# Moving the first tile's output projection out of the mixing block and into attention's last two steps

## The reference, cut to what matters

```
x = x + xattn(layernorm(x), ctx, ctx, Wq, Wk, Wv, Wo)   # 32 batches, 32 queries, 257 keys, 32 heads (8 kv heads), D = 1024
x = x + attn(layernorm(x), eta)                          # "mixing": softmax(max - y y^T) y, per batch, scaled by eta
x = x + ffn(layernorm(x), gate_w, expert_w)              # 8 experts, the best 2 for each token
# inside xattn, after the heads:
out = (probs @ v).reshape(32, 32, 1024)                  # called oT in the kernel, kept transposed
return out @ Wo                                          # 1024 x 1024, the projection that the change moves for the first 128 rows
```

## Time and profile before

| what | value |
|---|---|
| median of 3 runs | 1096.29 us (1095.58 to 1100.33) |
| the profiled execution, time | 1093.26 us |
| the profiled execution, span from first to last instruction | 1091.7 us |
| busy: PE, PEld, DVE, ACT, POOL | 1051.1, 964.5, 632.9, 477.7, 245.2 us |
| mean granted TensorE clock | 0.985 |
| block 1 ends, block 2 starts | 708.3 us |

### The profile page before, as it was taken

The page is one execution under the profiler, slowest core; times in us unless marked ns, Lnnn a source line. Parts: engine busy times, 40 slices in busy tenths (PEclk is TensorE's granted clock), DMA queues, the critical chain, the costliest instruction groups (busy, mean ns, idle before and its releaser), DMA issues. The chain is left out here.

```text
span 1091.7 us, 25345 instructions
## 1 busy us (share of the span) xinstructions
PE 1051.1 (96%) x9020; PEld 964.5 (88%) x9021; DVE 632.9 (58%) x1626; ACT 477.7 (44%) x1127; POOL 245.2 (22%) x414
## 2 busy tenths in 40 slices
PE   9999989999999999999999999499998799999996
PEld 9999889999999999999999999377776688888885
DVE  6641256666667666666667666648777635245220
ACT  4321245555555555554555554513323345355331
POOL 2000211211212121212112121024545333232232
PEclk9999999999999999999999999699999999999999
DMA  9442566575757565675657555464537588588432
GB/s 341 136 154 79 185 185 183 173 204 163 207 149 210 169 184 171 181 199 172 198 154 212 162 154 134 162 216 117 98 78 262 123 267 234 172 268 237 137 75 37
DMA packets 78602, 189.45 MB, mean 174 GB/s; under 512 B 16512, under 2 KB 27136, under 8 KB 74400
## 3 DMA queue, kind: packets, MB, share of 16 engines
q1 hardware_dynamic: 64096, 154.15, 45.4%
q0 software_dynamic: 14400, 33.88, 13.1%
HBM read 148.66 MB, written 44.56 MB: 177 GB/s over the span
## 5 line engine op out<-in xcount | busy, mean ns | idle before, releaser
L451 ACT ACTIVATE prob<-bank,nmax 128x257 f32<-128x257 f32 x256 | 122.0, 477 | 244.6 <-DVE nmax L590 244.4
L590 DVE TENSOR_REDUCE nmax<-bank 128x1 f32<-128x257 f32 x256 | 108.8, 425 | 160.2 <-PE bank L790 160.2
L670 PE MATMUL bank<-cT_h,wkv_h 128*128 128x256 f32 x512 | 155.0, 303 | 0.0
L679 PE MATMUL bank<-wkv_h,cT_h 128*128 128x256 f32 x512 | 154.4, 302 | 0.0
L670 PE MATMUL bank<-cT_h,wkv_l 128*128 128x256 f32 x512 | 145.0, 283 | 0.0
L670 PE MATMUL bank<-cT_l,wkv_h 128*128 128x256 f32 x512 | 144.7, 283 | 0.0
L679 PE MATMUL bank<-wkv_h,cT_l 128*128 128x256 f32 x512 | 144.5, 282 | 0.0
L679 PE MATMUL bank<-wkv_l,cT_h 128*128 128x256 f32 x512 | 143.9, 281 | 0.0
L345 POOL DMA_DIRECT2D qcat<-q_scratch x128 | 70.2, 555 | 271.6 <-PE bank L790 268.6
L705 PE MATMUL bank<-ident,prob 128*128 128x128 f32 x512 | 101.4, 280 | 10.0 <-DVE pT L245 6.8
L1640 PE MATMUL bank<-w_h,rows_h 128*128 x272 | 107.4, 395 | 0.0
(11 more groups left out here) (210 smaller groups left out, 2395.9 us busy)
## 6 DMA issues: line engine op xcount, KB each, us to landing
kcat<-k_scratch SPq DMA_DIRECT2D x128, 258.0 KB, 4.1
cx<-in_context SPq DMA_DIRECT2D x32, 1024.0 KB, 7.4
raw<-in_expert_w SPq DMA_DIRECT2D x48, 512.0 KB, 7.6
qcat<-q_scratch POOLq DMA_DIRECT2D x128, 128.0 KB, 3.2
k_scratch<-kT_h SPq DMA_DIRECT2D x32, 258.0 KB, 2.6
k_scratch<-kT_l SPq DMA_DIRECT2D x32, 258.0 KB, 3.0
x_in<-in_x SPq DMA_DIRECT2D x16, 512.0 KB, 6.2
expert_raw<-in_expert_w SPq DMA_DIRECT2D x16, 512.0 KB, 8.9
```

The lines of the kernel that those rows point to most:

```text
L451: act.activation(prob[:, 1 - par, s, 0:SK], s_ps[s % 2][:, 0:SK], ACT.Exp, bias=nmax[:, 1 - par, s:s + 1], accum_out=sums[:, 1 - par, s:s ...
L590: dve.reduce_max(nmax[:, 1 - par, s:s + 1], s_ps[s % 2][:, 0:SK], AXX, negate=True).then_inc(max_done, 1)
L670: o = pe.matmul(k_ps[:, j * 256:(j + 1) * 256], wkv[w][:, k, j * P:(j + 1) * P], cT[t][:, b % 2, k, :], start=(j == 0 and k == 0 and n == ...
L679: o = pe.matmul(v_ps[:, a * KV:(a + 1) * KV], cT[t][:, b % 2, k, a * P:(a + 1) * P], wkv[w][:, k, KV:2 * KV], start=(a == 0 and k == 0 and ...
```

## The change

1. TensorE makes `product` of tile 0 in block 1, in `first_product(k)`: chunk k of Wo is multiplied for both halves of the output at once (6 matmuls), one chunk in each of the slots (32, 3), (32, 4), (32, 5), (32, 6), (33, 0), (33, 1), (33, 2), (33, 3). Block 2 starts with tile 1.
2. The split of oT's tiles 0 and 1 (`ot_high`, `ot_low`) moves into block 1: tile 0 in (32, 1) on ScalarE and (32, 2) on VectorE, tile 1 in (33, 4) on both, behind the copy of the last batch into oT.
3. Wo's chunks 0 to 2 are loaded at step 28 and split in (30, 2), (30, 6), (31, 2) (ScalarE; VectorE a slot later). Chunks 3 to 7 are split in (32, 4), (32, 6), (33, 0), (33, 1), (33, 2).
4. For the last batch ScalarE copies five turned groups (1, 3, 4, 6, 7) instead of three.
5. The loads of x for tiles 0 and 1 move from SP's list in block 2 to the end of its list in block 1.
6. Buffers are laid out anew so that all this fits. The only waits that this adds to the steps before are one of GpSimd for `vl_zeroed` ahead of the first step.

The core of the diff:

```diff
+def turned_by_scalar(a):
+    return (1, 3, 4, 6, 7) if a == B - 1 else (1, 4, 7)
+def wo_step(c):
+    return ((B - 2, 2), (B - 2, 6), (B - 1, 2), (B, 4), (B, 6), (B + 1, 0), (B + 1, 1), (B + 1, 2))[c]
+def product_step(c):
+    return ((B, 3), (B, 4), (B, 5), (B, 6), (B + 1, 0), (B + 1, 1), (B + 1, 2), (B + 1, 3))[c]
...
 (SP, block 1)
+                if b == B - 4:
+                    for c in range(EARLY_WO):
+                        load_wo(c)
...
+            sp.wait_ge(v_done, B - 1)
+            for c in range(EARLY_WO, KC - 1):
+                load_wo(c)
+            for part in range(2):
+                sp.wait_ge(k_stored[part], 16 * B)
+            load_wo(KC - 1)
             sp.wait_ge(cT_done, 4 * B)
-            for c in range(KC // 2):
-                load_wo(c)
-            sp.wait_ge(v_done, B)
-            for c in range(KC // 2, KC):
-                load_wo(c)
+            for t in range(2):
+                sp.dma_start(sh.x_in2[:, t, :], x[t * P:(t + 1) * P, :]).then_inc(sh.x2_loaded[t], 16)
...
 (ScalarE, end of a slot)
-                    c = (b - B) * NG + s - 2
-                    if 0 <= c < KC:
-                        act.wait_ge(v_done, B)
-                        act.wait_ge(chunk_loaded[c], 32)
-                        act.activation(wo_s[0][:, c, :], wo_loaded(c), ACT.Copy).then_inc(wo_h_ready, 1)
+                    for c in range(KC):
+                        if wo_step(c) == (b, s):
...
+                            act.wait_ge(chunk_loaded[c], 32)
+                            act.activation(wo_s[0][c][:, :], wo_raw[c][:, :], ACT.Copy).then_inc(wo_h_ready, 1)
+                    if (b, s) in ((B, 1), (B + 1, 4)):
+                        t = b - B
+                        act.wait_ge(s_done, NG * (B - 1))
+                        act.activation(sh.ot[0][:, t, :, :], oT[:, t, :, :], ACT.Copy).then_inc(sh.ot_h_ready, 1)
...
 (VectorE, end of a slot)
+                    for c in range(KC):
+                        if wo_step(c) == (b, s - 1):
+                            dve.wait_ge(wo_h_ready, c + 1)
+                            dve.tensor_tensor(wo_s[1][c][:, :], wo_raw[c][:, :], wo_s[0][c][:, :].bitcast(F32), ALU.subtract).then_inc(wo_l_ready, 1)
+                    if (b, s) in ((B, 2), (B + 1, 4)):
+                        t = b - B
+                        dve.wait_ge(turned, NG * (B - 1))
+                        dve.wait_ge(sh.ot_h_ready, t + 1)
+                        dve.tensor_tensor(sh.ot[1][:, t, :, :], oT[:, t, :, :], sh.ot[0][:, t, :, :].bitcast(F32), ALU.subtract).then_inc(sh.ot_l_ready, 1)
...
 (TensorE)
+            def first_product(k):
+                if k == 0:
+                    pe.wait_ge(sh.ot_l_ready, 1)
+                    pe.wait_ge(cT_l_ready, 4 * B)
+                pe.wait_ge(wo_l_ready, k + 1)
+                for h in range(2):
+                    for m, (a, b) in enumerate(PASSES):
+                        o = pe.matmul(banks[h][:, :], sh.ot[a][:, 0, k, :], wo_s[b][k][:, h * 512:(h + 1) * 512],
+                                      start=(k == 0 and m == 0), stop=(k == KC - 1 and m == 2))
+                    if k == KC - 1:
+                        o.then_inc(sh.xo_done, 1)
...
+                    for c in range(KC):
+                        if product_step(c) == (b, s):
+                            first_product(c)
...
 (block 2)
-            load_x(0)
-            load_x(1)
...
-            ot_high(0)
             for t in range(NT + 2):
-                if t + 1 < NT:
+                if 1 <= t and t + 1 < NT:
                     ot_high(t + 1)
...
-            for t in range(NT):
+            for t in range(1, NT):
                 for unit in range(KC):
```

More of the change, by code:

```diff
@@ L65, in __init__ @@
         self.oT = self.at("oT", HIGH0, [P, NT, KC, P])
-        self.wo = [self.at("wo_h", HIGH1, [P, KC, D], F32R), self.at("wo_l", LOW1, [P, KC, D], F32R)]
+        place = lambda c: LOW1 + 8 * D * (c + 1) if c < EARLY_WO else LOW1 if c == KC - 1 else HIGH1 + 8 * D * (c - EARLY_WO)
+        self.wo = [[self.at(f"wo_{part}{c}", place(c) + i * 4 * D, [P, D], F32R) for c in range(KC)] for i, part in enumerate("hl")]
+        self.rows = [self.at("rows_" + part, STAGE + 16 * D + ROWS_AT + i * 8 * D, [P, 2, D], F32R) for i, part in enumerate("hl")]
+        self.ot = [part[:, :, :].rearrange("p a (c n) -> p a c n", n=P) for part in self.rows]
+        self.x_in2 = self.at("x_in2", STAGE, [P, 2, D])
+        self.x2_loaded = [sem("x2_loaded0"), sem("x2_loaded1")]
+        self.ot_h_ready, self.ot_l_ready, self.xo_done = sem("ot_h_ready"), sem("ot_l_ready"), sem("xo_done")
         self.w = [self.at("w_h", HIGH0, [P, 2 * SLOT], F32R), self.at("w_l", LOW0, [P, 2 * SLOT], F32R)]
@@ L182, in attend @@
         cT = [sh.at("cT_" + part, LOW0 + i * half, [P, 2, KC, 2 * P], F32R) for i, part in enumerate("hl")]
[L183 to L185 removed]
+        late = (nc.sbuf_base + 31) // 32 * 32 - sh.base
+        sb("late_map", [P, 4 * SKP + 8], F32)
+        zeros = sh.at("zeros", late, [P, 512])
+        kT = [sh.at("kT_" + part, at, [P, 2, 2, SKP], F32R) for at, part in zip((LOW1, late), "hl")]
+        wo_from = [LOW1 + 8 * D * (c + 1) + 4 * D for c in range(EARLY_WO)] + [LOW0, LOW0 + 4 * D, LOW0 + half, LOW0 + half + 4 * D, LOW1 + 4 * D]
+        wo_raw = [sh.at(f"wo_raw{c}", at, [P, D]) for c, at in enumerate(wo_from)]
         kvl = sb("kvl", [B, 2 * KV], F32)
         kl = [sb("kl_" + part, [P, 2, B], F32R) for part in "hl"]
[L189 removed]
         vl = sb("vl", [P, 2, KV], F32)
@@ L459, in _ @@
                     a = b - 2 if s < 2 else b - 1
-                    if i in TURNED_BY_SCALAR and (rest if s < 2 else heads):
+                    if i in turned_by_scalar(a) and (rest if s < 2 else heads):
                         copy_turned(act, act.copy, a, i)
@@ L606, in _ @@
                                           kT[0][:, par, :, 0:2 * P].bitcast(F32), ALU.subtract).then_inc(kT_l_ready, 1)
-                    if i not in TURNED_BY_SCALAR and (rest if s < 2 else heads):
+                    if i not in turned_by_scalar(a) and (rest if s < 2 else heads):
                         copy_turned(dve, dve.tensor_copy, a, i)
[L609 to L615, removed]
+                    for c in range(KC):
[7 more added lines that the diff above has]
+                        dve.tensor_tensor(sh.ot[1][:, t, :, :], oT[:, t, :, :], sh.ot[0][:, t, :, :].bitcast(F32), ALU.subtract).then_inc(sh.ot_l_ready, 1)
         @block.tensor
@@ L837, in finish @@
         first_raw = [sh.at("expert0_raw", LOW0, [P, KC, D]), sh.at("expert1_raw", LOW1, [P, KC, D])]
-        rows = [sb("rows_h", [P, 2, D], F32R), sb("rows_l", [P, 2, D], F32R)]
-        ot = [part[:, :, :].rearrange("p a (c n) -> p a c n", n=P) for part in rows]
-        gT = rows
+        ot, gT = sh.ot, sh.rows
         xg = sb("xg", [P, 2, D], F32)
```

46 lines of the change are left out of this document (27 added, 19 removed).

## The result

| | before | after |
|---|---|---|
| median, runs in turns on one chip | 1096.41 us (6 runs, 1092.54 to 1100.33) | 1090.51 us (6 runs, 1088.83 to 1092.94) |
| ratio | | 0.9943 [0.9922, 0.9964] |
| the profiled execution: time, span | 1093.26, 1091.7 us | 1090.4, 1088.8 us |
| mean granted TensorE clock | 0.985 | 0.993 |

What follows compares the result with a forecast made beforehand. TensorE, busy 1051.1 of 1091.7 us, was taken as the bound, with idle time in attention's tail. 14.2 - 4.1 - 1.8 - 0.5 - 1.5 = 6.3 less gave 1087.0 for the profiled execution, 1090 us as median; range 1085.5 to 1096.5.

Steps and rivals of the forecast that it cites:

- The first product, the two waits for VectorE: Attention's tail: chunk 0's product starts at 692.85; chunks 3 and 4 wait for VectorE's splits, at 700.0 and 704.2.
- The clock, 1.2 in the tail and 1.5 behind the border: TensorE falls to half clock near 694, costing 1.2 us, and once more behind the blocks' border, costing 1.5.
- The border: End of block 1: it comes at 712.4, 4.1 us later than before, with bounds of 711.2 to 713.6.
- `turn_y(0)` at 8.2 behind the border: Start of block 2: 6.4 without new waits, plus 1.8 (1.1 to 3.3) for the DMA of slots_cleared.
- The expert chunk: Block 2, ahead of products_of_rows(0): ScalarE's wait for the first expert load loses 0.5 us (0.4 to 3.1).
- The sum: All terms from the tail into block 2: 14.2 - 4.1 - 1.8 - 0.5 - 1.5 = 6.3 us less.
- What this mark gains, the kernel gains: Behind turn_y(0): every later piece hangs on TensorE or a chain of fixed length, so the whole gain stays.
- From one execution to the median: Whole kernel: the profiled execution's 1087.0 becomes a median of 1090 us, by the earlier median's 0.28% above its execution.
- Rival 1: Block 2 has no new wait and the clock stays: 10.1 us less, 1086 us; chance 0.15.
- rival 2: Block 2's waits for slots_cleared and the expert load both at upper bounds: 2.1 us less, 1094 us; chance 0.22.
- rival 3: Clock stays at 1.2 GHz through the tail, border 12.2 later: 1098 us; slower if over six of eight products; chance 0.07.
- rival 4: Loss ahead of the tail, by a split in (31, 0) or a later keys' DMA: up to 4 us each; chance 0.06.

Runs made afterwards that it cites:

- aligned: The changed kernel with rows_h and rows_l moved 896 bytes on, to a whole number of KB; against the kernel before: 1084.08 us, ratio 0.9910.
- experiment 4: aligned with chunks 0 to 2 of Wo split in slots (32, 2) to (32, 4) and chunk 3 in (32, 5); 1101.76 us, ratio 1.0030 to before.
- experiment 5: aligned with ScalarE copying three turned groups of the last batch instead of five; 1088.93 us, ratio 0.9909 to the kernel before.
- prod_back_al: aligned with tile 0's product back at the start of block 2, all else kept; 1095.96 us, ratio 0.9974 to the kernel before.
- Experiment 2: The changed kernel with GpSimd waiting for slots_cleared just before its first scatter, not before norm_y(0): 1088.99 us, ratio 0.9956 to before. A second kernel also moved copy_y(0).
- before_shifted: The kernel before with 128 unused bytes ahead of rows_h and rows_l, nothing else changed; 1099.85 us, ratio 1.0054 to the kernel before.
- scalar3_al: aligned with ScalarE copying three turned groups of the last batch, VectorE two more; 1088.93 us, ratio 0.9909 to the kernel before.

## Why the prediction was right, and where its steps were not

The time was met (1090.0 against 1090.51), and so was the order of events in the tail and at the border. That the number was met to 0.5 us is luck in part: two mistakes, of 2.7 us (the clock) and some 5 (the place of the row buffers), had opposite signs, and for the profiled execution the forecast was 1087.0 where 1090.4 was measured. By its own steps:

- **The first product, the two waits for VectorE.** Forecast 692.85, chunks 3 and 4. Measured 693.08, and those two chunks (0.16 and 0.63). VectorE's splits came sooner (wo_l of chunk 3 done at 698.6, forecast 700.0), since a slot's score did not wait for half-clock products.
- **The clock, 1.2 in the tail and 1.5 behind the border: wrong.** In the profiled execution the granted clock is 1.00 in all stretches from 694 to 724, through the idle 1.24 at the border and 2.14 ahead of `turn_y(0)`. The prediction weighed a rule and set it aside: transposes don't count as busy for the clock as other matmuls do (the Trainium skill, TensorE: Matmul & The Clock Gate, Part 4: PE-mode transpose). This trace agrees with it: with eight products between the same scores and transposes the clock stayed up. Two experiments bound that. In the fourth, with waits of 1.7 to 2.7 us ahead of the first four products, the clock was 0.50 to 0.62 in three of four stretches; in the fifth, with one wait longer by 0.33 than in aligned, it fell for some 3 us. A single trace doesn't show that this wait brought the fall, but it does show that the products alone don't keep the clock at 1.00.
- **The border: 4.1 later forecast, 3.1 measured** (3.3 from the values of step 32). The difference of 1.0 is the clock's 1.2, most of it. The lower bound, 711.2, was made for that case.
- **`turn_y(0)` at 8.2 behind the border: 8.9 measured.** The DMA landed 7.0 behind it, inside the 5.7 to 7.9. The prediction took most of the queue's hold-up away with the loads of x. The four gate loads were then issued in 2.25 in all, but the issue of eta, to which it gave no term, took 1.97. That is not a price of this load by itself: in prod_back_al, where SP's list is the same and TensorE and VectorE start block 2 otherwise, it took 0.58. What held it up is open.
- **The expert chunk: 0.5 forecast, next to nothing measured.** From `turn_y(0)` to the products are 3.9 us in the chain, where 3.6 were due by the earlier trace rows. Most of that difference is in how the chain cuts its pieces: by the first starts in the timelines it is 3.82 (720.33 to 724.15) against 3.73 (728.76 to 732.49). The chunk was issued at 716.20 and its split began at 721.75: 5.5, where the row chosen had 6.0.
- **What a first wait hides.** The 1.8 for slots and 0.5 for the chunk were added as if each stood alone. Experiment 2 shows that taking the first away gives back only 0.5 at `products_of_rows(0)`, since the second then ends last.
- **The sum.** At `products_of_rows(0)`: 732.56 before, 724.22 after, 8.3 less, where the sum had 6.3. The 2.0 are 1.0 at the border, 1.5 of clock behind it and 0.2 at the chunk, less the 0.7 by which `turn_y(0)` came later.
- **"What this mark gains, the kernel gains": the step that failed.** Edit 6 was described in front of the prediction, and it was given no cost. It costs 3.8 in the experts by the rows and 0.9 more in the tiles of block 2 (7.5 of the 8.3 are left at 816.57, 824.03 before), 0.5% by before_shifted and 0.3% between after and aligned. Nor is what follows of fixed length: from the last scatter of slots to the first 48 matmuls of the experts it was 38.9 and 40.5 us in two executions of the kernel before, and 38.9 to 41.8 in the six kernels with the product in the tail (41.0 in the changed kernel). In the four that moved rows_h by other steps or only what lies behind it, run on another chip, it was 43.9 to 45.5.
- **From one execution to the median.** The profiled executions differ by 2.9, the medians by 5.9. The one of before was 0.28% below its own median, that of after lies on its. 2.2 of this is seen between slots and experts, in DMAs (idx and xg). By the spread just named that is no more than executions differ by; it is not shown to be of the change.

Rival 1 was half right (the clock stays, 1.5 less), rival 2's waits were real but not at their upper bounds, rival 3's condition did not come: it took experiment 4, and for one product experiment 5, to bring it about. Nothing was lost ahead of the tail (rival 4).

## What to carry to other kernels

When buffers are laid out anew, compare the place of every operand of the longest matmul loop with before, and cost a changed remainder: here 128 bytes took a third to a half of what the change could bring. Work moved into an engine's idle time pays only if what it waits for is ready ahead of that time: prepared early, the product's 11.4 us lengthened the tail by only 2.5, and prepared in the same slots it made two engines take turns and the kernel slower than before. Behind a border of two blocks, list every wait that had slack before, in order: removing the first shows the second. And when a forecast hits, compare its steps all the same: this one hit with two terms wrong.

## What the runs showed of the hardware that was not expected

- Matmuls of 512 columns (fp32r) that follow each other without a wait start 0.227 us apart (10.90 for 48) with rows_h at its old place or 512 or 1,024 bytes further on; 0.232 (11.15) at 128 bytes; 0.234 (11.21) at 64. TensorE is busy for 60.00 of 60.00 us from 930 to 990 at a granted clock of 1.00 both before and after, so neither a wait nor the clock goes with it.
- The issue of one load of 128 single elements (eta) behind four small gate loads took 1.97 us of SP's queue, where the loads of 512 KB behind it were issued in 4.52 for eight. In the six kernels with the product in the tail it took 1.66 to 1.99, in prod_back_al, with the same list in SP, 0.58.
- The clock held 1.00 through idle times of 1.24 and 2.14 us between stretches of products in the changed kernel. In scalar3_al it fell for some 3 us behind waits of 0.49, 1.18 and 0.63 us, where aligned, with 0.16, 1.18 and 0.63, kept it.
